# Gather indices copied for four chunks at once, one chunk ahead, in a graph network layer

## The reference

```python
q = (x @ Wq).reshape(n, 8, 16)
x_dst = x[edge_dst]                       # a gather for each edge
wk, wv = mlp2(edge_features, ...), mlp2(edge_features, ...)
k = tensor_product(x_dst, edge_sh, wk, Cqk)   # w * sum_s sh[:, s] * (x_dst @ C[:, s, :]), 9 values of s
v = tensor_product(x_dst, edge_sh, wv, Cv)
attn = einsum('ehd,ehd->eh', q[edge_src], k)  # a second gather for each edge
# softmax over the edges of a node, weighted sum of v, W_out, W_self, batch norm
```

## Time and profile before

| | |
|---|---|
| median of 3 runs | 5317.2 us (5316.74 to 5322.68) |
| profiled execution | 5320.04 us |
| its span, first to last instruction | 5318.1 us |
| mean granted TensorE clock | 0.963 of full speed |
| busy over the span | PE 91%, PEld 85%, DVE 76%, POOL 71%, ACT 64% |
| bytes moved by DMA | 1006 MB, mean 189 GB/s |

### The profile page before, as it was taken

The page is one execution under the profiler, slowest core; times in us unless marked ns, Lnnn a source line. Parts: engine busy times, 40 slices in busy tenths (PEclk is TensorE's granted clock), DMA queues, the critical chain, the costliest instruction groups (busy, mean ns, idle before and its releaser), DMA issues. The chain is left out here.

```text
span 5318.1 us, 116347 instructions
## 1 busy us (share of the span) xinstructions
PE 4829.7 (91%) x35582; PEld 4517.3 (85%) x35582; DVE 4062.1 (76%) x5044; ACT 3416.6 (64%) x6495; POOL 3756.6 (71%) x3788
## 2 busy tenths in 40 slices
PE   7999999999999999999999999999999999998256
PEld 6888899898899898899999889998988988988243
DVE  5878788787788887787888888787877878887335
ACT  2666666666666666666666666666666666666237
POOL 3777777777777777777777777777777777775370
PEclk9999999999999999999999999999999999999578
DMA  8898889889889998898988989898889989897320
GB/s 214 190 201 200 201 198 202 199 202 200 197 198 199 203 203 197 198 201 199 203 202 200 202 199 204 196 202 202 199 197 200 202 199 203 200 204 163 95 72 25
DMA packets 693459, 1006.46 MB, mean 189 GB/s; under 512 B 120054, under 2 KB 378168, under 8 KB 693160
## 3 DMA queue, kind: packets, MB, share of 16 engines
q1 hardware_dynamic: 574856, 753.93, 62.0%
q0 software_dynamic: 112960, 242.16, 21.3%
q10 hardware_dynamic: 5600, 9.83, 0.6%
HBM read 826.64 MB, written 178.93 MB: 189 GB/s over the span
## 5 line engine op out<-in xcount | busy, mean ns | idle before, releaser
L814 PE MATMUL psum<-chi,zhi 128*128 128x256 f32 x7840 | 2339.0, 305 | 1.7 <-DVE rv L720 1.5
L525 POOL DMA_INDIRECT gq<-qtab,idxs x1568 | 1838.2, 1172 | 478.0 <-issue 478.0
L817 PE MATMUL psum<-clo,zhi 128*128 128x256 f32 x7840 | 2148.7, 283 | 0.0
L520 POOL DMA_INDIRECT gx<-in_xg,idxs x1568 | 1549.5, 988 | 697.1 <-issue 374.1
L816 PE MATMUL psum<-chi,zlo 128*128 128x256 f32 x6272 | 1778.2, 284 | 0.0
L814 PEld LDWEIGHTS psum<-chi,zhi 128*128 128x128 f32 x7840 | 1498.0, 191 | 103.5 <-issue 103.5
L817 PEld LDWEIGHTS psum<-clo,zhi 128*128 128x128 f32 x7840 | 1496.2, 191 | 0.0
L674 DVE TENSOR_TENSOR z<-psum,shb 128x1536 f32<-128x1536 f32 (+1 forms) x784 | 1131.1, 1484 | 391.6 <-PE psum L786 381.5
L569 ACT ACTIVATE zhi<-z 128x1536 fp32r<-128x1536 f32 (+1 forms) x784 | 994.4, 1268 | 471.1 <-DVE z L674 464.4
L816 PEld LDWEIGHTS psum<-chi,zlo 128*128 128x128 f32 x6272 | 1200.0, 191 | 102.8 <-issue 102.8
L699 DVE TENSOR_TENSOR zlo<-z,zhi 128x1536 fp32r<-128x1536 f32 (+1 forms) x784 | 922.4, 1218 | 0.0
(11 more groups left out here) (210 smaller groups left out, 6555.5 us busy)
## 6 DMA issues: line engine op xcount, KB each, us to landing
shb<-in_shT SPq DMA_DIRECT2D x392, 640.0 KB
shb<-in_shT SPq DMA_DIRECT2D x392, 512.0 KB
rows<-ot SPq DMA_DIRECT2D x392, 416.0 KB
e<-in_eT SPq DMA_DIRECT2D x392, 128.0 KB
drow<-rankd SPq DMA_DIRECT2D x392, 128.0 KB
gx<-in_xg,idxs POOLq DMA_INDIRECT x1568
gq<-qtab,idxs POOLq DMA_INDIRECT x1568
qtab<-qs ACTq DMA_DIRECT2D x25, 256.0 KB, 5.7
```

Source lines behind the costliest of these rows:

```text
L520: nc.gpsimd.indirect_dma_start(out=gx[:, s, k, :], out_offset=None, in_=xg[:, :], in_offset=bass.IndirectOffsetOnAxis(ap=idxs[:, s, k:k + ...
L525: nc.gpsimd.indirect_dma_start(out=gq[:, s, k, :], out_offset=None, in_=qtab[:, :], in_offset=bass.IndirectOffsetOnAxis(ap=idxs[:, s, TC + ...
L814: mm(tpb[:, k, :], zhi[:, s, j, e], chi[:, j, :], start=(j == 0), stop=False)
L817: last = mm(tpb[:, k, :], zhi[:, s, j, e], clo[:, j, :], start=False, stop=(j == ST - 1))
```

## The change

The index buffer `idxs` has two halves of 32 columns in place of four slots of 8. A new function `indices(g)` copies the 32 columns of a whole group of four chunks. It is called once ahead of chunk 0, and then in the last chunk of every group (`c.r % GC == GC - 1`) for the next group, ahead of that chunk's own gathers. The wait for the copy is in the first chunk of a group only, and asks for the copy of that group. The gathers take their indices from `ids`, the chunk's eight columns in the group's half.

```diff
-            idxs = ms("idxs", [P, 4, 2 * TC], i32)
+            idxs = ms("idxs", [P, 2, GC * 2 * TC], i32)
...
+                    def indices(g):
+
+                        nc.gpsimd.tensor_copy(idxs[:, g.r // GC % 2, :],
+                                              idx_all[:, bass.ds(g.value() * 2 * TC, GC * 2 * TC)]).then_inc(idx_made, 1)
+
                     def gathers(c):
                         s = c.slot(4)
                         if c.old(4):
...
                             pool.wait_ge(wkq_done, c.value() - 3)
                             pool.sem_inc(pool_passed, 1)
-                        nc.gpsimd.tensor_copy(idxs[:, s, :], idx_all[:, bass.ds(c.value() * 2 * TC, 2 * TC)]).then_inc(idx_made, 1)
-                        pool.wait_ge(idx_made, c.value() + 1)
-                        pool.sem_inc(pool_passed, 1)
+                        if c.r % GC == GC - 1 and (c + 1).there():
+
+                            indices(c + 1)
+                        if c.r % GC == 0:
+                            pool.wait_ge(idx_made, c.turn(GC) + 1)
+                            pool.sem_inc(pool_passed, 1)
+                        at = c.r % GC * 2 * TC
+                        ids = idxs[:, c.r // GC % 2, at:at + 2 * TC]
                         for k in range(TC):
                             nc.gpsimd.indirect_dma_start(
                                 out=gx[:, s, k, :], out_offset=None, in_=xg[:, :],
-                                in_offset=bass.IndirectOffsetOnAxis(ap=idxs[:, s, k:k + 1], axis=0),
+                                in_offset=bass.IndirectOffsetOnAxis(ap=ids[:, k:k + 1], axis=0),
                             ).then_inc(x_in[s], 16)
                         for k in range(TC):
                             nc.gpsimd.indirect_dma_start(
                                 out=gq[:, s, k, :], out_offset=None, in_=qtab[:, :],
-                                in_offset=bass.IndirectOffsetOnAxis(ap=idxs[:, s, TC + k:TC + k + 1], axis=0),
+                                in_offset=bass.IndirectOffsetOnAxis(ap=ids[:, TC + k:TC + k + 1], axis=0),
                             ).then_inc(q_in[s], 16)
 
+                    indices(Chunk(0, 0))
                     gathers(Chunk(0, 0))
                     gathers(Chunk(0, 1))
```

## The result

The changed kernel takes 5039.4 us (median of 4 runs, 5024.8 to 5049.8) beside 5319.9 us of the kernel before: ratio 0.947, interval 0.944 to 0.950. The profiled execution took 5049.8 us, the slowest of the four, span 5047.8. The forecast of 5087 was on the right side and 48 us too high; the range, 4990 to 5150, holds the time.

The account below looks back on a forecast made before the run. GpSimd's queue, 12.31 us a chunk, was taken as the bound; less 0.82, plus 0.10 gives 11.59, raised to 11.72 for gathers held by VectorE. 392 chunks save 231 us: 5089, or 5087 beside the median; range 4990 to 5150.

Parts of the forecast that it names:

- GpSimd is the bound, with TensorE's waits the other side of it: Main loop: GpSimd's queue sets 12.31 us a chunk with no wait for others; TensorE waits 199.9 us for gathered features.
- 0.82 us taken away, 0.10 added: GpSimd's queue, per chunk: copy 0.315 and wait 0.811 go, 0.305 ahead of the first gather comes; group copy adds 0.10.
- Holds tie GpSimd to VectorE: Gathers last 1.07 us a chunk beyond their unheld 0.948 us each, held by VectorE, so GpSimd is clocked by VectorE's cycle.
- A gather that would end inside L699 is held until it is over: GpSimd gathers beside VectorE's subtraction of two SBUF tiles: up to 2.36 us long, VectorE not held in turn.
- A pace of 11.72 us, between 11.59 and 11.85: GpSimd's new time a chunk, the middle of two values; GpSimd still the bound, 5045 to 5137 us, chance 0.38.
- GpSimd ahead: Rival: GpSimd leads by more than its jitter, TensorE's 11.49 us a chunk is left, 4996 beside the median; chance 0.28.
- 33 operations at eight in a cycle of 11.49 us: Four chunks need 32 feature and query gathers and one row gather; at eight in a VectorE cycle, 11.85 us a chunk.
- TensorE's own pace of 11.49: TensorE's time a chunk without waits, from four chunks in a row lasting 45.95 us; nothing was to move on TensorE.
- The plain sum, 5035: Rival: GpSimd's queue is the sum of its parts, holds fixed at 1.07 us; 11.59 us a chunk, chance 0.14.
- A lead is used up or kept: GpSimd's waits for a free slot, four chunks back: at most 4.0 us, absent until GpSimd leads by more than now.

Follow-up runs that it names:

- the two runs with the PSUM input: VectorE's subtractions at L699 and L708 (L710 and L719 in the changed kernel) read their first input from PSUM: kernel before 4991 us, changed kernel 5010 us.
- the second trace of the changed kernel: The changed kernel run again unaltered: median 5024.7 us, runs 5018.9 to 5075.3; the traced execution took 5019.9 us, TensorE busy throughout from 500 us on.
- the old places: The changed kernel with `idxs` allocated last and a dummy of the old size in its place, so all other tiles lie as before: 5059 us, ratio 0.9525.

## Why the prediction was right, and where it was off

- *GpSimd is the bound, with TensorE's waits the other side of it*: right. Taking 0.51 us a chunk out of its queue brought 198 us, and taking its holds away 323.
- *0.82 us taken away, 0.10 added*: right. Taking the wait away brought 198/392 = 0.505 us a chunk, as one term of the sum had it, though by the luck told above. A group copy took 31.1/86 = 0.36 us, where 0.4 was taken: 0.09 us a chunk, 0.12 with the little wait behind it. The copy's median rose from 201 to 225 ns for 24 more columns, so the figure of the Trainium skill ("GPSIMD Engine Reference", section 3.1), 0.02 us, agrees.
- *Holds tie GpSimd to VectorE*: right, by the two runs with the PSUM input. The prediction set this against the Trainium skill ("SBUF — State Buffer", section "Who interferes with whom"), and that was half of what the section says. It does say that `tensor_tensor` did not stall the making of descriptors, and for these indirect gathers the traces show otherwise. But it also says that a VectorE instruction with two SBUF inputs contends with a GpSimd instruction that reads SBUF, and a gather reads its indices there; the runs agree with that.
- *A gather that would end inside L699 is held until it is over*: too simple. Of the two gathers that it was read from, the one at 2509.84 is no case of it. It ended at 2511.16, inside L699, and 0.82 us behind the end of L695, which reads two SBUF tiles too and had started ahead of it. In the trace before, 125 gathers started in the last 0.12 us ahead of L699 and ended inside it, after 0.94 to 1.02 us. The 302 that started 0.16 to 1.22 us into it all ended behind it. So the hold depends on where in the gather VectorE's instruction falls; which part of a gather that is was not taken apart. The row of L695:

```profile
2509.64 0.69 DVE L695 TENSOR_TENSOR hidlo<-hid,hidhi 128x512 fp32r<-128x512 f32 x1 [1.58 <-ACT hidhi L590]
```

- *A pace of 11.72 us, between 11.59 and 11.85*: right for the first part of the profiled execution, 11.70. The step that failed is that it would hold to the end. The prediction set "GpSimd ahead" apart as another case, at 4999; the run was both, 11.70 to some 2830 us and 11.53 after it, and its time lies between. That 11.72 came so near to the first part is luck too: it was the middle of two values, taken for want of a reason, and in the second trace of the changed kernel there is no such part behind 500 us. The count behind it (33 operations at eight in a cycle of 11.49 us) was too simple. In the second part, where TensorE has no wait, the cycles last from 11.2 to 12.0 us, and the longer ones mostly take nine or ten.
- *TensorE's own pace of 11.49*: 11.53, since the edit moves tiles; with the old places it was 11.46. The prediction had said that nothing moves on the other engines. By itself that is 392 x 0.04 = 16 us; in the whole it was no loss, as the old places showed.
- *The plain sum, 5035*, was nearest to the time (5039), and its pace, 11.59 us, is the mean of the whole stretch, but by accident: it is 0.11 us below that of the first part and 0.06 above that of the second, and the holds that it took as fixed went from 1.07 to 1.26 us a chunk.
- *A lead is used up or kept*: the waits for a free slot, taken at nothing, stayed so (1.5 us in all).

## What to carry to other kernels

An engine that the page shows 75% busy can be the bound: add its busy time to the idle time that nothing but itself ends. A copy and a wait for it in such a queue cost the wait most, and making the copy one step ahead takes that off without any saving of copies. Where two queues run at nearly the same pace, a head start for the one that feeds the other (here TensorE began 6.6 us later, once) can take off waits for the whole run; in the kernel before, whose queue was 0.8 us a chunk slower than TensorE, the same head start did nothing. Where one engine's operations take longer at some times than at others, look in order of time at what the other engines run beside them: here the holds were worth more than the whole change.

## What the runs showed of the hardware

A gather on GpSimd that takes 0.945 us unheld took up to 2.36 us in the rows above beside VectorE's subtractions of two SBUF tiles. The means of the two groups were 1175 and 988 ns in the kernel before; they fell to 976 and 967 ns there, and to 947 and 945 ns in the changed kernel, when the first input of these subtractions came from PSUM. VectorE's subtraction took the same time either way, 1751 and 1750 ns. A copy on GpSimd, the wait for it and a gather behind it left 0.81 us of idle time; with the copy made a chunk earlier it was 0.16. Moving all tiles behind `idxs` by 128 bytes a partition lengthened TensorE's chunk of 92 products from 11.62 to 11.69 us. A transfer started by ScalarE inside the loop went with stops of up to 5.4 us on that engine, 211.5 us in all; what they are made of was not looked into.
